# Layer 2's feed-forward: the activation engine rounds the four weight slabs of chunk 0 in one run, ahead of the second norm half

## The reference, cut to what matters

```python
x = x + _L2_ffn_ref(_layernorm(x, axis=-1), L2_ffn_w_gate_up, L2_ffn_w_down)

def _L2_ffn_ref(h_shard, w_gate_up, w_down):
    gate_up = jnp.einsum('bsh,oh->bso', h_shard, w_gate_up)
    gate, up = jnp.split(gate_up, 2, axis=-1)
    h = jax.nn.silu(gate) * up
    out = jnp.einsum('bsi,hi->bsh', h, w_down)
    return out
```

## Time and profile before

| | us |
|---|---|
| median of 3 runs | 2280.16 |
| the 3 runs | 2278.24 to 2282.38 |
| time of the profiled execution | 2278.32 |
| its span, first to last instruction | 2276.4 |
| mean granted clock of PE over the span, as a share of full | 0.956 |

### The profile page before, as it was taken

The page is one execution under the profiler, slowest core; times in us unless marked ns, Lnnn a source line. Parts: engine busy times, 40 slices in busy tenths (PEclk is TensorE's granted clock), DMA queues, the critical chain, the costliest instruction groups (busy, mean ns, idle before and its releaser), DMA issues.

```text
span 2276.4 us, 39262 instructions
## 1 busy us (share of the span) xinstructions
PE 2057.6 (90%) x14719; PEld 1662.9 (73%) x14719; DVE 1057.5 (46%) x2393; ACT 910.0 (40%) x1740; POOL 503.2 (22%) x358
## 2 busy tenths in 40 slices
PE   7989999877997889977789999899978999799996
PEld 7967776875456778764577777799968999755554
DVE  5556666653113456688536666323333555411111
ACT  3356666332223445576634454322243222222221
POOL 3323331312433111000311110223241110023332
PEclk9999999998997999989899999999999999999998
DMA  3200000326544111121110000222220000489995
GB/s 119 81 14 27 26 28 29 103 97 245 89 81 145 42 65 65 71 117 41 55 33 18 27 14 2 79 56 65 65 73 23 27 26 1 158 266 325 321 320 143
DMA packets 91367, 203.91 MB, mean 90 GB/s; under 512 B 9194, under 2 KB 14414, under 8 KB 89070
## 3 DMA queue, kind: packets, MB, share of 16 engines
q1 hardware_dynamic: 79790, 175.06, 23.5%
q0 software_dynamic: 11424, 26.75, 5.7%
HBM read 184.08 MB, written 21.43 MB: 90 GB/s over the span
## 4 chain that ended last, share of the span: by engine, by line
PE 67%; DMA 11%; DVE 10%; ACT 5%; issue 5%; POOL 1%; SPq 0%; DVEq 0%; ACTq 0%; POOLq 0%
PE psum L106 15%; PE psum L109 13%; PE psum L107 13%; DMA l3f_sum_dram<-l3f_y,l3f_rows 9%; PE psum L901 3%; PE psum L3497 3%; PE psum L3465 2%; PE psum L2691 2%; PE psum L3483 2%; PE psum L927 1%; PE psum L2114 1%; PE psum L2341 1%; DVE l2x_highest L2196 1%; PE psum L2706 1%; PE psum L1535 1%
## 5 line engine op out<-in xcount | busy, mean ns | idle before, releaser
L1535 PE MATMUL psum<-l3f_gate_up,l3f_x_turned 128*128 128x352 f32 x496 | 155.0, 466 | 0.8 <-ACT l3f_x_turned L1594 0.8
L1535 PEld LDWEIGHTS psum<-l3f_gate_up,l3f_x_turned 128*128 128x128 f32 x496 | 93.3, 193 | 48.5 <-issue 2.5
L2155 ACT ACTIVATE l2x_probs<-psum,l2x_shift 100x361 f32<-100x361 f32 x128 | 65.0, 560 | 96.9 <-DVE l2x_shift L2200 95.5
L1810 POOL TENSOR_TENSOR l2x_ctx_lo<-l2x_ctx_raw,l2x_ctx_hi 128x1448 fp32r<-128x1448 f32 x8 | 26.4, 3296 | 328.1 <-ACT l2x_ctx_hi L1818 328.0
L106 PE MATMUL psum<-xn_hi,l2f_w_gu_hi 128*128 128x400 f32 x256 | 90.2, 352 | 9.1 <-ACT l2f_silu L594 5.2
L3636 ACT ACTIVATE l0x_probs<-l0x_probs,l0x_lowest 100x361 f32<-100x361 f32 x128 | 75.2, 589 | 42.1 <-DVE l0x_lowest L3800 42.1
L107 PE MATMUL psum<-xn_lo,l2f_w_gu_hi 128*128 128x400 f32 x256 | 89.2, 348 | 0.0
L1510 POOL DMA_INDIRECT l3f_sum_dram<-l3f_y,l3f_rows x31 | 49.2, 1587 | 180.9 <-DMA l3f_sum_dram<-l3f_y,l3f_rows 145.8
L1620 DVE TENSOR_TENSOR l3f_h<-l3f_silu,psum 128x352 f32<-128x352 f32 x31 | 16.2, 521 | 152.7 <-ACT l3f_silu L1607 152.7
L1561 PE MATMUL psum<-l3f_down,l3f_h_turned 128*128 128x512 f32 x186 | 85.1, 593 | 0.8 <-DVE l3f_h_turned L1626 0.8
L449 POOL TENSOR_TENSOR l2f_w_gu_lo<-l2f_raw_gu,l2f_w_gu_hi 128x512 fp32r<-128x512 f32 x32 | 43.1, 1356 | 190.2 <-ACT l2f_w_gu_hi L464 190.2
(11 more groups left out here) (534 smaller groups left out, 6143.9 us busy)
## 6 DMA issues: line engine op xcount, KB each, us to landing
l3f_gate_up<-in_slabs_dram SPq DMA_DIRECT2D x31, 1280.0 KB, 7.9
l3f_down<-in_slabs_dram SPq DMA_DIRECT2D x31, 512.0 KB, 5.3
l0x_w_raw<-in_slabs_dram SPq DMA_DIRECT2D x52, 256.0 KB, 2.7
l0f_weights<-in_slabs_dram SPq DMA_DIRECT2D x8, 1536.0 KB, 17.0
l1x_piece<-in_bit_w_dram SPq DMA_DIRECT2D x8, 1024.0 KB, 6.9
l1f_raw<-in_bit_w_dram SPq DMA_DIRECT2D x8, 1024.0 KB, 9.0
l2f_raw_gu<-in_slabs_dram SPq DMA_DIRECT2D x32, 256.0 KB, 2.7
l3f_down<-in_slabs_dram SPq DMA_DIRECT2D x31, 192.0 KB, 7.1
```

Source lines behind the costliest of these rows:

```text
L1535: mm = pe.matmul(c.psum[:, bank + x, 0:self.INNER], self.x_turned[:, t % 2, k, :], self.gate_up[:, q, at:at + self.INNER], start=k == 0, s ...
L2155: act.activation(self.probs[:, m % 2, g, :], c.psum[0:S, g, 0:C], ACT.Exp, bias=self.shift[:, g:g + 1], scale=self.SCALE).then_inc(self.s( ...
```

## The change

ACT's part of the stage, `Ffn.act`. Before, ACT rounded slab 0, then worked through the second norm half with slab 1 rounded inside it (by the hook), and rounded slabs 2 and 3 behind it. Now it rounds slabs 0 to 3 one after another and then does the whole second norm half, with no hook. No instruction is added or removed. Only this stage uses `Ffn.act`; the other feed-forwards have their own.

```diff
     def act(self, c, act):
         act.wait_ge(c.sem("residual_ready"), self.index + 1)
         self.act_before_std(c, act)
-        ffn_high_gu(c, act, self, 0, 0)
-        half_act(self.norm, act, 1, lambda: ffn_high_gu(c, act, self, 0, 1))
-        for j in range(1 if len(half(self.norm, 1)) == 2 else 2, self.gu_slabs):
+        for j in range(self.gu_slabs):
             ffn_high_gu(c, act, self, 0, j)
+        half_act(self.norm, act, 1)
         self.prepare_act(c, act)
         ffn_act(c, act, self)
```

## The result

The changed kernel takes 2267.57 us (median of 6 runs, 2266.27 to 2270.20) against 2279.02 us for the kernel before on the same chips (6 runs, 2276.47 to 2282.38). The ratio is 0.9953, with a 95% interval of 0.9943 to 0.9963: between 8 and 13 us faster. The forecast was 2268.5 us.

A forecast was written before the change was run, and what follows sets the result against it. PE is full from 1475 to 1650 us, so only its waits in the stage's opening can give. Slab 2 starting 10.4 us earlier plus 1.3 of clock gives 11.7: 2280.16 - 11.7 = 2268.5 us, range 2264.5 to 2273.

The forecast's parts named there:

- The two waits: Stage opening: PE's idles of 2.45 us ahead of slab 1 and 5.22 us ahead of slab 2 both go.
- the third: PE's third opening wait, 5.22 us until ACT's first Silu has read slab 0's banks; forecast hidden with 1.1 us over.
- The ladder: Slabs 2 and 3, POOL's low parts, SP's down load, down roundings, table, Silu: POOL's last low part moves 11.8 us earlier.
- The norm's delay, priced at 0: ACT's second norm half: three moved roundings take 1.56 of an idle 1.62 us, so no delay; fully serial, 0.27.
- the norm slips: Rival: POOL beside DVE's statistics slows the norm, PE's restart slips up to 1.3 us, 1.6 with serial roundings; 2270; chance 0.12.
- The signs of being wrong: PE idle over 0.3 us ahead of slab 2, deviation starting after 1436.3, or new waits from 1475 on.
- only the shift would meet POOL: By the skill page, only DVE's norm shift, a small instruction, would meet POOL here; no run so far shows it.
- The clock: PE's full clock through the opening gains 1.3 us on 48 matmuls; rival that it still falls once: 2270 to 2271, chance 0.23.
- The sum: Slab 2 starting 10.4 us earlier plus 1.3 us of clock: 11.7 us, so 2268.5 us against the median.
- Only the first wait goes: Rival: the down load or table comes late for another reason; 5.1 us gained alone, 2275 us; chance 0.05.
- Does nothing that lasts: Rival: a later stage gives back the gain, within 0.2%; 2280 us; chance 0.02.
- slower, by the clock: Rival: small shifts behind 1460 us add 33 us more at half clock; 2285 us or above; chance 0.02.

The follow-up runs named there:

- the three experiments on it: Old-order kernel with three extra POOL subtractions (1.0001); changed kernel with POOL waiting for DVE's shift (0.9954); changed kernel with one-tensor-input shift operations (0.9962).
- the three built on it: Changed kernel with POOL waiting for DVE's shift (2268.05 us), with one-tensor-input shifts (2268.31), or with POOL waiting and down roundings behind the first two Silus (2266.61).
- one kernel: Kernel before, old slab order, with chunk 0's down roundings moved behind the first two Silus: 2271.72 us (0.9966), again 2273.21 us (0.9970).
- POOL's wait: Changed kernel, with POOL taking slab 2's low part only after DVE has written the norm's first shift: 2268.05 us, ratio 0.9954.
- the second timing: Changed kernel timed again unaltered, against the kernel before: 2267.26 us, ratio 0.9960.
- the first experiment: Half of the change on the kernel before: ACT rounds slabs 0 and 1 ahead of the second norm half, 2 and 3 behind: 2275.39 us, ratio 0.9985.

## Why the prediction was right

**The two waits.** Both are gone, as forecast. PE does not idle ahead of slab 1 or slab 2. The first is worth 5.12 us up to the restart when it goes alone (5.1 forecast), the third 6.76 of the stage when it goes alone (6.5 expected). The two add: 5.12 + 6.76 = 11.88, which is what the stage gains with POOL kept out of the norm's way (219.68 - 207.80). By the stages alone it is 4.24 + 6.76 = 11.00, since the first half gives 0.88 back at the idle that it leaves. The ladder ran as worked out: in the changed kernel the down load goes out at 1437.60, 6.18 behind the first rounding (6.2 forecast), and Silu waits for PE.

**The norm's delay, priced at 0.** This is the term that was off. ACT's four roundings did fit into the idle 1.62 us: the deviation came 2.25 us behind the first rounding, as before. But the norm slipped by 0.92 us at DVE's shift, one step further. It was named as the rival *the norm slips*, with 0.12 and up to 1.6 us, and the cause given there, POOL working beside DVE, is what the three experiments on it show. Its price there was worked out from a slowed POOL and did not come that way: POOL's four ran at 1.25 each. The rival and the forecast both came true in part: the restart was forecast 10.1 us behind the first rounding, came at 11.01, and comes at 10.08 as soon as POOL keeps out of the way. The signs of being wrong looked at the deviation and at the idle ahead of slab 2, both of which were as forecast, and not at the shift between them. Two smaller errors on this path nearly cancel: slab 1 began 1.01 us into the first back-transposes and not behind their 1.23, and the gap ahead of the restart was 1.34 and not 1.20.

The sentence there that only the shift would meet POOL was right. I counted it as small by its own 0.16 us, where the price is the rest of POOL's running instruction. And that no run had shown it was wrong, as was the statement ahead of the prediction that the engines meet only at semaphores. The trace of the kernel before shows this wait in other stages, as in these rows of DVE and POOL:

```profile
707.86 0.97 DVE L164 SCALAR_TENSOR_TENSOR ln_shift<-ln_moments,ln_inverse 100x2 f32<-100x2 f32 x1
```

```profile
707.53 1.29 POOL L1778 TENSOR_TENSOR l1x_w_lo<-l1x_w_raw,l1x_w_hi 128x512 fp32r<-128x512 f32 x1 [2.18 <-ACT l1x_w_hi L1783]
```

The shift ends at 708.83, POOL at 708.82. Of the 35 shifts in that trace 25 ran with POOL at rest and took 0.16 us; the other ten ran beside a subtraction of POOL and took 0.28 to 1.15, each ending within 0.05 us of POOL's running instruction. With a shift in the middle of POOL's run, a delay of up to 1.0 us (1.15 in place of 0.16) could have been read before the change was made. The slow subtractions of the earlier trace rows have the same cause the other way round: in this stage the seven of 1.57 to 1.59 us each start while DVE takes the low part of `l2f_h` from two tensors in SBUF, with 0.42 to 0.43 us of that still to run, and all others take 1.26 to 1.30.

**The clock.** Right: it stays at full through the remaining gap, in the changed kernel and in the three built on it. For slabs 2 and 3 I took 1.3 us. In the changed kernel the two products both wait for PE and start 8.72 us apart, at 1447.17 and 1455.89, which is 48 matmuls; before, these took 10.35 less 0.17 of drain, so the term measures about 1.5. It rests on one profile of the kernel before; two profiles of one kernel differed by 2.8 us in what the clock cost behind the same idles.

**The sum.** 11.7 forecast, 10.95 in the opening: slab 2 starts 15.47 us behind the first rounding (1446.89 - 1431.42) instead of 25.04, which is 9.6 for the forecast's 10.4, and the clock's term adds 1.5 for its 1.3; with the 0.92 taken out by POOL's wait it is 11.88. Over the steady part nothing is given back. The time by ratio is 10.7 us lower (8.4 to 13.0), by medians 11.45; the second timing gives 9.1 by ratio. That the time itself came within 1 us of 2268.5 is in part luck: the kernel before had a median of 2279.02 in this timing, 1.1 us below the 2280.16 that the forecast started from, which is more than the norm's 0.9.

**The other rivals.** *Only the first wait goes* is what the first experiment builds, and it gives 4.2 us; the change does more. *Does nothing that lasts* and *slower, by the clock* did not occur, though single profiles do spread by 6 us behind this stage.

## What to carry to other kernels

Follow a late load back through its issuing queue: here a load waited for POOL's work on slabs that nobody needed yet, and an in-order engine made an unrelated Silu wait for it. To learn whether two waits on one engine's path add, take each away alone, as half of the change, and compare the sum with the whole. When work is moved to make one engine's stream dense, look at what short instructions another engine runs meanwhile, price them by the long instruction that may hold them, and look in the trace for another place where the two already meet.

## What the runs showed of the hardware

A DVE operation with two tensor inputs from SBUF did not finish before POOL's running subtraction had: 1.08, 1.07, 0.64, 0.63 and 0.56 us in place of 0.16 in this stage of five runs, and ten times in other stages of the kernel before (0.28 to 1.15 us), each ending within 0.05 us of the end of a POOL instruction. It did not wait for the whole of POOL's run: in the changed kernel it ended with the third of four. A reciprocal and a pair of one-column operations with one tensor input ran beside POOL at their usual length. The Trainium skill, "GPSIMD Engine Reference", Key points, says that POOL shares its SBUF interfaces with VectorE and names DVE instructions with two SBUF inputs among those that contend with it. These traces agree, with 1.08 us against 0.16. In the other direction a subtraction of POOL that started beside such a DVE operation took 1.57 to 1.59 us in place of 1.26 to 1.30.

Behind the same two idles of PE (2.45 and 1.20 us) one kernel restarted at the full clock in one execution (granted clock 1.00 from 1450.60) and ran at half for some 6 us in another (0.50 from 1452.50); its stage was 2.8 us longer there.
